# One-hot products for expert 0's last rows, centred turning, ranks from logits, and an earlier third turning in a cross-attention and mixture-of-experts kernel

## What is computed

```python
x = x + xattn(layernorm(x), ctx_768)   # 16 heads of 64, softmax over 256 keys, w_o, b_o
x = x + ffn(layernorm(x))

# ffn: N = 4096 tokens, E = 8 experts, capacity 640, top 2
logits = x_flat @ router_w + router_b
gates = softmax(logits)
expert_mask = one_hot(top_k(gates, 2)).sum(1)
pos = cumsum(expert_mask, axis=0) - 1
valid = expert_mask * (pos < capacity) > 0
buf[e, pos] += x_flat              # the rows of each expert, in order of tokens
h = gelu(einsum('ecd,edh->ech', buf, w1) + b1)
out = einsum('ech,ehd->ecd', h, w2) + b2
y = sum over the chosen experts of gates * out[e, pos]
```

## Time and profile before

| | |
|---|---|
| median of 3 runs | 1016.76 us |
| the profiled execution | 1014.67 us |
| its span | 1012.9 us |
| TensorE busy | 971.7 us, 96% |
| VectorE busy | 770.1 us, 76% |
| ScalarE busy | 624.0 us, 62% |
| GpSimd busy | 280.1 us, 28% |
| weight loads w1, issue to landing, median of 8 | 7.9 us |

### The profile page before, as it was taken

One profiled execution on the slowest core, in us unless ns is written; L12 is line 12 of the kernel. 1 busy time (PEld: TensorE's weight loads), 2 busy tenths in 40 slices (PEclk: granted clock), 3 DMA queues, 4 the chain that ended last, 5 costly groups with the idle time before them and its releaser, 6 DMA issues. The chain is left out here.

```text
span 1012.9 us, 23424 instructions
## 1 busy us (share of the span) xinstructions
PE 971.7 (96%) x8496; PEld 881.0 (87%) x8496; DVE 770.1 (76%) x2090; ACT 624.0 (62%) x1736; POOL 280.1 (28%) x438
## 2 busy tenths in 40 slices
PE   8989999999999999999999999999979999999996
PEld 7778888888888888888888888888768999999995
DVE  6897768888787888878797888878745666776662
ACT  5777767777776767777686777677614333344330
POOL 4542021314123231403223131411251333222233
PEclk9999999999999999999999999999979999999998
DMA  8440101101010101101010110001105543454522
GB/s 239 142 119 2 33 2 33 33 23 53 13 42 15 33 13 33 45 2 44 12 32 6 33 31 11 17 5 43 65 18 178 137 102 80 108 131 127 137 27 27
DMA packets 48432, 56.76 MB, mean 56 GB/s; under 512 B 5324, under 2 KB 44218, under 8 KB 48192
## 3 DMA queue, kind: packets, MB, share of 16 engines
q1 hardware_dynamic: 39488, 46.30, 14.7%
q0 software_dynamic: 8832, 8.98, 5.5%
HBM read 36.01 MB, written 24.20 MB: 59 GB/s over the span
## 5 line engine op out<-in xcount | busy, mean ns | idle before, releaser
L847 ACT ACTIVATE prob<-psum,negmax 128x256 f32<-128x256 f32 x512 | 238.7, 483 | 80.0 <-DVE negmax L1004 80.0
L797 ACT ACTIVATE probt<-psum 128x512 f32<-128x512 f32 x256 | 157.3, 616 | 57.2 <-PE psum L657 55.1
L1004 DVE TENSOR_REDUCE negmax<-psum 128x2 f32<-128x512 f32 x256 | 160.0, 682 | 22.8 <-PE psum L641 22.6
L1015 DVE TENSOR_SCALAR prob<-prob,invtot 128x256 f32<-128x256 f32 x512 | 166.8, 389 | 4.5
L657 PE MATMUL psum<-ident,prob 128*128 128x128 f32 x1024 | 150.3, 273 | 3.0 <-DVE prob L1015 3.0
L926 ACT ACTIVATE hid<-psum,b1t 128x640 f32<-128x640 f32 x64 | 50.9, 795 | 134.4 <-PE psum L574 134.4
L657 PEld LDWEIGHTS psum<-ident,prob 128*128 128x128 f32 x1024 | 119.2, 140 | 13.2 <-issue 4.7
L671 PE MATMUL psum<-probt,v 128*64 128x256 f32 x1024 | 124.6, 385 | 0.0
L514 POOL DMA_INDIRECT slot_table<-row,picki x64 | 65.5, 1023 | 192.8 <-DVE picki L1117 166.6
L550 POOL DMA_INDIRECT out_rows<-y,rowi x40 | 65.6, 1640 | 175.6 <-DVE y L1167 153.4
L847 ACT ACTIVATION_READ_ACCUMULATOR prob<-psum,negmax 128x1 f32 x512 | 110.5, 216 | 0.0
(11 more groups left out here) (158 smaller groups left out, 2731.2 us busy)
## 6 DMA issues: line engine op xcount, KB each, us to landing
w1r<-in_w SPq DMA_DIRECT2D x8, 1024.0 KB, 7.9
w2r<-in_w SPq DMA_DIRECT2D x8, 1024.0 KB, 10.1
slot_table<-blank SPq DMA_DIRECT2D x8, 662.5 KB, 9.9
rows<-slot_table SPq DMA_DIRECT2D x7, 662.5 KB, 5.3
xin<-in_x SPq DMA_DIRECT2D x16, 256.0 KB, 3.0
out_rows<-x SPq DMA_DIRECT2D x16, 256.0 KB
c<-in_ctxt SPq DMA_DIRECT2D x16, 128.0 KB, 3.1
c<-in_ctxt SPq DMA_DIRECT2D x32, 64.0 KB, 2.9
```

The lines of the kernel that those rows point to most:

```text
L797: copy = lambda dst, src, **kw: act.activation(dst, src, ACT.Copy, **kw)
L847: last = act.activation(prob[:, m % 2, u, qb, :], psum[:, u, qb * S:(qb + 1) * S], ACT.Exp, bias=negmax[:, m % 2, u, qb:qb + 1], accum_out ...
L1004: dve.tensor_reduce(negmax[:, m % 2, u, :], psum[:, u, :].rearrange("p (q s) -> p q s", q=ST), AX.X, ALU.max, negate=True).then_inc(sem("m ...
L1015: last = dve.tensor_scalar(prob[:, m % 2, u, qb, :], prob[:, m % 2, u, qb, :], invtot[:, m % 2, u, qb:qb + 1], None, ALU.mult)
```

## The change

1. *Loop.* In every fourth quarter (r = 3) `turn2` and `copy2` stand behind `turn1` and `copy1`, ahead of `exp3` and `v`. In second quarters (r = 1) `ln2_stats` and `ln2_root` stand behind `q` and the normalising.
2. *Ranks.* `compare` compares the logits (with bias) instead of the gates, in all batches; `shift` writes into `lshift`, so that the logits stay.
3. *Batch 15.* Statistics and centring per half: rows less their mean go to `row`, are turned in two parts (`x2t_part`) and give logits (`logits_part`); `bias` multiplies by the inverse root. ScalarE scales the rows afterwards (`scale`).
4. *Expert 0.* Its rows aren't read back after the last scatter. SP loads what batches 0 to 13 scattered (`load_base`), `base` multiplies it with the identity in fp32 into banks 0 to 3, and `spread` adds the rows of batches 14 and 15 by products of their high and low parts with one-hots (`onehot`: slot number equal to key). `gathered` makes `bufh` and `bufl` of it. Of expert 0's rows in the table only the nine columns behind the values are loaded. Both batches are scattered nevertheless, for the other experts; batch 15's `pick` stands behind `gathered`.
5. *Expert 1.* Its rows are turned in `down(0)` instead of `up(0)`, behind slices 0 to 2.
6. The end of the timeline is written as one list per engine; all `warm` in it is gone. GpSimd's list has `iota`, `row_lo` and w2's low part behind the last scatter. Other banks for `up` (6, 7 and 2, 3) and for `turn_rows` (0, 1).

The diff, cut:

```diff
         if r == 1 and 2 <= b:
-            out += steps("ln2_stats ln2_root", b - 2) + steps(q, m + 1) + steps(half[1], m - 1)
+            out += steps(q, m + 1) + steps(half[1], m - 1) + steps("ln2_stats ln2_root", b - 2)
...
-        out += steps("turn1 copy1", m - 1) + steps("exp3 v", m)
+        out += steps("turn1 copy1", m - 1) + (steps("turn2 copy2", m - 1) if r == 3 else []) + steps("exp3 v", m)
...
+    out += [*steps("max0 max1 max2 max3", m), ("slot", c - 1), ("a_lo", m - 2), *steps(half[1], m - 1), ("q_lo", z),
...
+            *steps("bias compare shift rank slot high onehot gate", d), ("x2add", o0), ("stat", o0),
+            ("x2add", o1), ("stat", o1), ("center", o0), ("center", o1), *steps("keys pick", d),
+            *steps("bias compare rank shift slot high onehot gate keys", e)]
+    out += [("iota", 0), ("scatter", c - 1), ("ln2_root", d), ("scatter", c), ("row_lo", d), ("ln2_root", e),
+            ("row_lo", e), ("scatter", d), ("scatter", e), ("w_lo", 2), ("w_lo", 3)]
...
+            def load_base():
+
+                for r in range(3):
+                    sp.wait_ge(sem(f"scatter{r}"), 16 * 2 * ST * ((B - r) // 3))
+                sp.wait_ge(sem("turn"), UNITS * (PERIODS - 1))
+                sp.dma_start(base_rows, table[0:CAP, 0:D].rearrange("(s p) w -> p s w", p=P))\
+                  .then_inc(sem("base_in"), 16)
...
+            def base(_):
+
+                pe.wait_ge(sem("base_in"), 16)
+                pe.wait_ge(sem("x2t_sb"), B - 1)
+                pe.wait_ge(sem("biased"), B - 1)
+                pe.wait_ge(sem("slots"), B - 1)
+                pe.wait_ge(sem("x2t_part_sb"), ST)
+                for half in range(2):
+                    for kk in range(DC):
+                        for s in range(ET):
+                            lo, hi = max(s * P, half * HALF), min((s + 1) * P, (half + 1) * HALF)
+                            if lo < hi:
+                                pe.matmul(psum[:, GATHER[half][kk], lo - half * HALF:hi - half * HALF],
+                                          base_rows[:, s, kk * P:(kk + 1) * P], ident[:, lo - s * P:hi - s * P],
+                                          start=(lo == half * HALF), stop=False)
+
+            def spread(n):
+
+                at, half = divmod(n, 2)
+                pe.wait_ge(sem("onehot"), at + 1)
+                pe.wait_ge(sem("row_lo"), at + 1)
+                for kk in range(DC):
+                    for t in range(ST):
+                        for j, a in enumerate((spread_hi[at], spread_lo[at])):
+                            mm = pe.matmul(psum[:, GATHER[half][kk], 0:HALF], a[:, t, kk * P:(kk + 1) * P],
+                                           onehot[at][t][:, half * HALF:(half + 1) * HALF], start=False,
+                                           stop=(at == 1 and t == ST - 1 and j == 1))
...
+            def center(n):
+                b, t = divmod(n, ST)
+                dve.wait_ge(sem("stat"), t + 1)
+                dve.wait_ge(sem(f"scatter{b % 3}"), 16 * 2 * ST * (b // 3))
+                dve.tensor_scalar(row[:, b % 3, t, 0:D], x2[:, b % 2, t, :], mean_var["ln2"][:, t, 0:1], None,
+                                  ALU.subtract).then_inc(sem("centered"), 1)
...
-            for u in range(TURNS):
-                turn_rows(0, u)
+            for half in range(2):
+                gathered(half)
+            pick_(B - 1)
             for e in range(NE):
                 for j in range(HC):
                     split_hid(HC * e + j)
-                    if e + 1 < NE and j in TURN_AFTER:
+                    if 1 <= e < NE - 1 and j in TURN_AFTER:
                         turn_rows(e + 1, TURN_AFTER.index(j))
```

More of the change, by code:

```diff
@@ L103, in timeline @@
         if 3 <= b:
-            out += {0: steps("gate_exp gate", b - 3), 3: steps("pick scatter", b - 3)}.get(r, [])
+            out += {0: steps("gate_exp gate compare", b - 3), 3: steps("pick scatter", b - 3)}.get(r, [])
         if r == 1 and 2 <= b:
@@ L784, in down @@
                     mm.then_inc(sem("down"), 1)
-            pe.wait_ge(sem("slots"), B)
-            for u in range(TURNS):
-                turn_rows(0, u)
+                    if e == 0 and s < TURNS:
+                        turn_rows(1, s)
             for e in range(NE):
@@ L1093, in slot_, with high, onehot_ @@
                    .then_inc(sem("slots"), 1)
+            def high(b):
+                dve.wait_ge(sem("slots"), b + 1)
+                dve.scalar_tensor_tensor(highkey[:, :, :], slot[:, :, :], 1.0, valid[:, :, :], ALU.add, ALU.mult)\
+                   .then_inc(sem("high"), 1)
+            def onehot_(b):
+                at = b - (B - 2)
+                dve.wait_ge(sem("high"), at + 1)
+                dve.wait_ge(sem("scores"), UNITS * PERIODS)
+                dve.wait_ge(sem("iota"), 1)
+                for t in range(ST):
+                    last = dve.tensor_scalar(onehot[at][t], numbers, highkey[:, t, 0:1], None, ALU.is_equal)
+                last.then_inc(sem("onehot"), 1)
             def keys(b):
                 dve.wait_ge(sem("slots"), b + 1)
+                dve.wait_ge(sem("gates"), b + 1)
                 for t in range(ST if b + 1 < B else 0):
@@ L1129, in _ @@
                          norm3=lambda m: norm(m, 3),
[L1130 removed]
+                         ln1_stats=ln1_stats, ln2_stats=ln2_stats, ln2=ln2, bias=bias, shift=shift, gate=gate, compare=compare,
+                         high=high, onehot=onehot_, stat=stat, center=center, rank=rank_, slot=slot_, keys=keys, pick=pick_)
             for stage, n in TIMELINE:
```

230 lines of the change are left out of this document (159 added, 71 removed).

## The result

The changed kernel takes 1009.97 us, the median of 6 runs (1009.70 to 1010.65), against 1016.62 us for the kernel before beside it (6 runs, 1015.82 to 1018.58): a ratio of 0.9931, 95% interval 0.9921 to 0.9942. It is faster by 6.65 us. The prediction was 998.0 with a range from 992 to 1005, so the sign was right and the size was not: 12 us are missing. The profiled execution took 1009.70 us with a span of 1008.0.

What follows compares the result with a forecast made beforehand. TensorE, 98.87 of 100 us busy in attention, left only short waits and the 28.4 us chain to the first up. Loop 9.1 + end 9.6 = 18.7 us off 1014.67 gives 996.0; median 2.1 above: 998.0, range 992 to 1005.

Steps and rivals of the forecast that it cites:

- Loop, third turning: Fourth quarters of the loop: moving turning and copy ahead ends 15 waits of the next quarter's scores, 7.15 us.
- the forecast of the whole loop: Attention loop: 7.15 us from the moved turning plus 1.97 us from the moved statistics, summed to 9.1 us.
- the four waits (1.97 us): Second quarters: third turning waits four times for normalised probabilities; moving the ln2 statistics was to end this, 1.97 us.
- Loop, statistics: Second quarters: ln2 statistics behind the normalising gain 1.97 us; the later GpSimd root hides in VectorE's third-quarter idle time.
- the loop's waits only move: Rival, loop: next quarter waits 0.45 us elsewhere, so the loop gives 0 to 2 us, median 1005 to 1007; chance 0.11.
- Last quarters, nothing: End of the loop: reordered batch 13 and 14 work costs nothing; last output product stays near 737.4, within 1 us.
- Centred rows at 740.8: Behind the last output product: VectorE has batch 15's rows centred at 740.8 us, ready for turning.
- Base at half clock, 4.3 us: Ahead of expert 0: TensorE's 12 fp32 base products take 4.3 us at half clock, 2.1 at full clock.
- First `up`: Start of expert 0: first up product at 753.7 us, 12.1 us earlier, between 750.5 and 756; loop gain not included.
- What is given back: Expert 0 to expert 1: later scatters, w2's low part and w1's load leave 9.6 of 13.7 us won.
- the forecast's chain: down(0): w1 loads behind w2's low part, VectorE splits it before adding bias, third slice waits from 775.0 to 777.5.
- The splits of `hid`: Expert 0: GpSimd's w2 split beside VectorE's splits might stall up by one to two us; not in the sum.

Runs made afterwards that it cites:

- e2_before_turn: The kernel before with only the third turning and its copy moved ahead of the fourth exp and v in fourth quarters: 1006.59 us, ratio to before 0.9894.
- e1_stats_ahead: The change with the ln2 statistics and inverse root put ahead of q and the normalising again in second quarters: 999.27 us, ratio to before 0.9825.
- f1_stats_wlo: The change with the ln2 statistics ahead of q again and w2's low part on VectorE instead of GpSimd: 997.31 us, ratio to before 0.9850.
- g2_add_ahead: f1_stats_wlo with VectorE's additions, statistics and centring ahead of batch 14's one-hots, and batch 14's pick behind batch 15's count: 993.16 us, ratio to before 0.9779.
- f4_warm_late: f1_stats_wlo with 32 warming products in TensorE's wait behind the last output product: 994.89 us, ratio to before 0.9834.
- h2_w1_ahead: g2_add_ahead with 32 warming products, gelu's table early, expert 1's w1 loaded ahead of the scatters' wait, its rows ahead of b2: 992.18 us, ratio to before 0.9750.
- h3_no_wlo: g2_add_ahead with w2's low part back on GpSimd behind the scatters: 997.20 us, ratio to before 0.9800.

## Why the prediction was wrong, step by step

- **Loop, third turning: mechanism right, size too low.** None of the 15 waits of the joints is left, and nothing took their place. The forecast was 7.15 us; with the turning alone quarter 62's scores start at 691.70 in `e2_before_turn` and at 691.07 in `e1_stats_ahead`, against 700.15: 8.5 to 9.1 us. That is the forecast of the whole loop, 9.1: the moved turning also ended the four waits (1.97 us) that the sum had given to the statistics. So the sum of the loop could be had by one of its two edits.
- **Loop, statistics: the step that failed.** The move of the `ln2` statistics behind the normalising stood at +1.97 us, with the cover "hidden by the idle times VectorE has in the third" quarter. Measured: 10.7 us the other way. VectorE does idle ahead of `kl`, but in wait for ScalarE, which is late by the same chain: 0.53 us ahead of `al` with the late root (above) and 0.53 us without it. So this idle time took nothing up, and TensorE needed the bank of `kl` 0.17 us after it was ready. I asked who waits for `ln2` and not who waits for what stands behind `ln2` on VectorE. This step alone, put right, gives 999.27 us, within 1.3 us of the forecast. The rival "the loop's waits only move" gave the loop 0 to 2 us, and 0.2 was measured. That is luck: it had the joint's own waits moving, `e2_before_turn` shows that they don't, and the new ones come from the other edit.
- **Last quarters, nothing: wrong by 1.2 to 1.3 us.** From quarter 63's scores to the last output product it takes 24.7 us before, 26.0 in the change, 25.9 in `e1_stats_ahead`. TensorE waits 1.1 us for `chosen` of batch 14, since `pos` stands ahead of the last output products, and 0.9 us for `al`. But it waited 2.0 us for `al` before, so these two are no loss. New is a wait of 0.74 us at 718.87 for which the profile shows no releaser. `f1_stats_wlo` doesn't have it and takes 24.6 us, as before. Where it comes from stays open.
- **Centred rows at 740.8: late.** Turning them was to start 3.4 us behind the last output product and starts 4.3 behind it (4.5 in `e1_stats_ahead`). VectorE's chain of small steps wasn't done when the last product was: its key took 1.04 us for 16 columns beside GpSimd's `row_lo`. `g2_add_ahead`, which puts the additions ahead of the one-hots, makes it 2.6.
- **Base at half clock, 4.3 us: the clock right, the size helped by luck.** It took 4.69 us in the change, and the clock was back at full speed from 750.1 us on, ahead of its end. Wholly at half clock it takes 5.49 (`f1_stats_wlo`), at full clock 2.94 (`f4_warm_late`), where I had 4.3 and 2.1. The Trainium skill (FP8 and Floating Point Precision, TensorE Precision Notes) has four passes for a true fp32 product. The 2.94 us measured lies nearer to my 2.1, which agreed with that, than to the 1.1 us of the turnings' rate. So the trace leans to the page; no run counts the passes.
- **First `up`: 12.1 us earlier than the last output product alone would have it, measured 10.5.** 28.4 us became 17.9.
- **What is given back: 2.5 us, measured 3.3, by another road.** w2's low part was through 14.6 us behind the first `up`, as forecast (768.3 - 753.7), w1 was issued 14.7 us behind it. But the third slice didn't wait for y: the splits of `hid` held `down(0)` first, and the clock fell. With the splits freed the forecast's chain appears (1.05 us in `f1_stats_wlo`), and `h2_w1_ahead` shows what it is worth in a quicker kernel, 2.9 us by the stretch.
- **The splits of `hid`: named, but not in the sum.** I had written that no row shows w2's split beside them. Now one does: a split of 0.83 us takes 2.91, one of 0.49 takes 2.69, and the second ends at 772.64, 0.36 us behind GpSimd's two pieces (772.28). The Trainium skill (SBUF — State Buffer, two separate sides) says that the loser waits for the other's whole instruction and doesn't share; the trace agrees. I had put "one to two us" beside the sum and not into it; 1.0 to 1.8 was measured.

Of the 13.8 us by which the span missed the forecast (18.7 less 4.9), 11.2 are the difference of the spans with and without the moved statistics (1008.0 and 996.8). Of these, 9.9 us are there at the first `up`, and 1.3 come in `down(0)`, where the clock fell in one and not in the other; that the statistics brought this fall about isn't shown. The other 2.6 are 1.2 us in the last quarters and 1.9 on the way to the first `up`, less 0.5 that were given back less than forecast.

## What to carry to other kernels

- Before you move a step behind another to fill an idle time, follow its engine's queue to the next step that another engine waits for, data or bank, and read how much room is there. A step with 0.17 us of room showed in no list of waits here.
- Where TensorE was busy 99% of the time, a wait had two prices: what the list says (0.47 us) and what a batch got longer by (0.78 us). Take the difference between two starts of the same step.
- When a chain is shortened, list what starts at its end. Here the loads started where the last scatter landed, and 0.7 to 1.6 us of the gains ahead of them were paid back until w1 went first and the rows went ahead of b2. With w2 moved ahead as well, the scatters landed late, and there was no gain.

## What wasn't expected of the hardware

- A 128x16 operation on VectorE took 1.04 us and another 0.80 us in the change, beside GpSimd's subtractions of 512 columns, where they take 0.17 us otherwise. Both ended within 0.05 us of GpSimd's instruction.
- The clock fell in `down(0)` of the change, behind two gaps of 0.64 and 0.65 us, and not in `e1_stats_ahead` or `h3_no_wlo` behind two gaps of the same length. What told them apart stays open.
- The kernel before differs by up to 5.8 us between sets of runs (medians 1012.0 to 1017.8), the four runs of `h2_w1_ahead` by 0.75 us. Nothing was tried to find out why.
